# Scores of a chunk moved ahead of the query projection in TensorE's step of a pipelined attention and feed-forward stack

## The chip, the cores and the metric

One core of one Trainium2 chip runs the whole program; the other cores do nothing. Its engines are TensorE (PE, matrix products; PEld is its weight load), VectorE (DVE), ScalarE (ACT), GpSimd (POOL) and SyncE (SP, which only issues DMAs here). The metric is the device time of one execution in microseconds (us), median of the runs, all inputs and outputs in HBM.

## What is computed

`x` is 2048 tokens by 128 features, f32. Four residual layers follow each other: a causal attention (A), a stack (S0), a grouped attention (B), and the same stack again with the same weights (S1). Each stack has depth 6, and each of its layers is, cut to what matters here:

```
for i in range(6):
    x = attn_layer(shift_tokens(x), ...) + x     # 16 heads of 64, windows of 32 tokens, each query
    x = ffn_layer(shift_tokens(x), ...) + x      # window looks at its own and the one before
attn_layer: q, k, v = split(x @ Wqkv); q, k = l2norm * scale, then rotated; k cached per window
            out = softmax(8 q k^T, masked) v;  out @ Wo
ffn_layer:  a, gate = split(layernorm(x) @ W1 + b1);  a * gelu(gate) @ W2 + b2
```

## The kernel before, in words

Features lie on the partitions, tokens on the free axis. A stack works in **chunks** of 128 tokens (16 to a layer, 96 to a stack) and **blocks** of 512 tokens for the feed-forward part (24 to a stack). Every engine runs the same list of steps `k`: 16 written out, a hardware loop over layers 1 to 5 with 16 steps in its body, and some steps at the end that drain the pipeline (`read_steps`, L361). In each step every engine works at several chunks in different stages: `at.chunk(d)` is the chunk `k - d`, or nothing if there is none; `at.block(d)` is a block that falls due in every fourth step. The order in which an engine takes the pieces is written out by hand in its `step`, and each piece begins with waits on counting semaphores; so an engine that waits holds back everything behind that wait.

TensorE's step (L544) is, in the order before:

1. pieces of the feed-forward blocks that come first (L559 to L588), the product with `Wo` of chunk k-4 (L590), more feed-forward pieces (L599 to L616);
2. transposing the probabilities of chunk k-3 into `slot[1]` (L618 to L624; the row names it `slot<-consts,probs` at L538, the line of the helper `turn`);
3. in every fourth step the third gate tile (L626 to L631), in another fourth step the product with `W2` (L633 to L644, the matmuls are L642);
4. the **query projection** of chunk k (L646, `project_in`, matmuls L531 to L533) into `slot[0]`;
5. in every fourth step a value tile (L655), in another the mean of a block (L662, matmul L665);
6. the **value products** of chunk k-3: 128 small matmuls (L668 to L681, matmuls L677);
7. the **scores** of chunk k-2 into `slot[3]`: two matmuls that lay down the mask (L700) and 128 small ones (L707), behind the waits L685 to L697;
8. transposing the rotated queries (L713, L538), the value projection (L719), transposing the attention output `Os` (L726), the key projection (L734), transposing the rotated keys (L742).

Each fourth step of one kind has one piece of the feed-forward part that touches `slot[3]`, and the scores wait for the engine that empties it. Below the four kinds of step are called by that piece: the **variance step** (L565 at its head; the scores wait for `ln_eps`, L689), the **W2 step** (piece L641; they wait for `ln_half` and `f_done`, L691 and L695), the **gelu step** (gates L607, L609, L631; they wait for `gelu_done`, L693) and the **mean step** (L665; they wait for `hid_done`, L697).

The engines that answer to it:

- ScalarE (`act_stack`, L752): copies of `slot[2]` and `slot[1]` to `qT`, `V`, `OT`; `k_copy` (L817); `Exp` of the scores (L822); `kT` (L832); `probsT` (L845); in the gelu step a table load and three `Gelu` (L858, the rows name the whole group `centred<-slot,b`); then `q_copy` (L871).
- VectorE (`dve_stack`, L973): row maximum of the scores (L1001), cosine half of the queries straight from `slot[0]` (L983, signals `aq_done`), normalising the keys (L987), subtracting the maximum (L1021), sums of squares (L1028, L1081), cosine half of the keys, row sums (L1050), residual add (L1063), in the W2 step `XA` (L1114, signals `f_done`), normalising the queries (L987, signals `qn_done`), in the mean step the rotation tables (L1094), `x_lo` (L1130), and last `Os` (L1138, signals `on_done`), which takes the value products from `slot[1]`. The next row maximum stands directly behind `Os`.
- GpSimd: the sine halves (L909), the add to the rotated queries (L925), the inverse norms (L938, L942).
- SyncE copies the values of each chunk into window form (`VW<-V`, L452 to L456) by DMA.

The value projection (L723) and the transpose of `Os` (L728) wait for `on_done`; the key projection (L739) waits for `aq_done`; the query projection of the next step waits for `k_copy` and `ak_done`.

Of the kernel before, what the change touches and what calls it, by code (L numbers as in the profile page):

```python
# [23 lines left out]
NCH = S // 128  # L24
NB = S // 512
DEPTH = 6
H, DH = 16, 64
WIN = 32
# [4 lines left out]
START = 1  # L33
# [57 lines left out]
def build(nc, A, out, place, stages=("A", "S0", "B", "S1")):  # L91
    n_const = A["shape_constants"].shape[1]
    ctx = ExitStack()
    with ctx:
        def sem(name):
            return ctx.enter_context(nc.semaphore(name))

        def sb(name, shape, dt=F32, at=ctx):
            return at.enter_context(nc.sbuf_tensor(name, shape, dt))
# [4 lines left out]
        def const(name):  # L104
            a, n = place[name]
            return consts[:, a:a + n]

        ident = const("ident")
        ident_b = sb("ident_b", [128, 128], BF16)
        mask_qk = sb("mask_qk", [128, 128], BF16)  # L110
        mask_kq = sb("mask_kq", [128, 128], BF16)
        mask_win = sb("mask_win", [128, 2, 2 * WIN], BF16)
# [11 lines left out]
        slot = [ctx.enter_context(nc.psum_tensor(f"slot{i}", [128, 1024], F32)) for i in range(4)]  # L124
# [88 lines left out]
        qT = sb("qT", [128, 8, 128], F32, mem)  # L213
        kT = sb("kT", [128, 8, 160], F32, mem)
# [29 lines left out]
        s = {n: sem(n) for n in names}  # L244
# [126 lines left out]
        class Stage:  # L371
# [13 lines left out]
            def upto(self, c):  # L385
                return self.g + min(max(c + 1, self.lo), self.hi)

            def blocks(self, c):
                return self.f + min(max(c + 1, self.lo), self.hi) // 4
# [129 lines left out]
        def norms_before(call):  # L519

            return (1 + (LN_S0 if call == 0 else LN_S1)) * NB - BLOCKS * call

        def pe_stack(pe, call):
            n0 = norms_before(call)
# [19 lines left out]
            def step(layer, g, f, k, lo, hi):  # L544
                at = Stage(g, f, k, lo, hi)
                upto, blocks = at.upto, at.blocks
# [13 lines left out]
                if b is not None:  # L560
# [4 lines left out]
                    for c in range(4):  # L565
                        mm = pe.matmul(slot[3][:, 512 + c:513 + c], squares[:, 0, c * 128:c * 128 + 128],
                                       const("mean1"), start=True, stop=True)
# [10 lines left out]
                if b is not None:  # L578
# [4 lines left out]
                    for c in range(4):  # L583
                        at_col = 4 * (b % 4) + c
                        mm = pe.matmul(slot[3][:, 128 * c:128 * c + 128],
                                       rstd[:, at_col:at_col + 1].to_broadcast([128, 128]), ident,
                                       start=True, stop=True)
                    mm.then_inc(s["ln_bc"], 1)  # L588

                c = at.chunk(4)  # L590
                if c is not None:
# [3 lines left out]
                    for j in range(8):  # L595
                        mm = pe.matmul(slot[2][:, 512:640], Wo[:, j, :], OT[:, j, :], start=(j == 0), stop=(j == 7))  # L596
# [21 lines left out]
                c = at.chunk(3)  # L618
# [15 lines left out]
                if b is not None:  # L634
# [6 lines left out]
                    for t, (j, a, m) in enumerate(VALUE_TILES):  # L641
                        mm = pe.matmul(slot[3][:, 512:1024], W2[0:m, j, :], hidden[0:m, j, :],  # L642
                                       start=(t == 0), stop=(t == 2))
                    mm.then_inc(s["w2_mm"], 1)  # L644

                c = at.chunk(0)  # L646
                if c is not None:
                    if c == 0:
# [14 lines left out]
                if b is not None:  # L663
                    pe.wait_ge(s["xb_done"], START + 2 * upto(k - 4))
                    pe.matmul(slot[2][:, 512:1024], const("centre128"), XB[:, (b % NB) * 512:(b % NB) * 512 + 512],  # L665
                              start=True, stop=True).then_inc(s["ln_mean"], 1)

                c = at.chunk(3)  # L668
                if c is not None:
# [3 lines left out]
                    for h in range(H):  # L673
                        r = slice(64 * (h % 2), 64 * (h % 2) + 64)
                        col = (h % 2) * 512 + (h // 2) * 64
                        for w in range(4):
                            mm = pe.matmul(slot[1][32 * w:32 * w + 32, col:col + 64],  # L677
                                           probsT[r, h // 2, 32 * w:32 * w + 32],
                                           VW[c % 2][r, w, (h // 2) * 64:(h // 2) * 64 + 64],
                                           start=True, stop=True)  # L680
                    mm.then_inc(s["pv_mm"], 1)  # L681

                c = at.chunk(2)
                if c is not None:
                    pe.wait_ge(s["qT_sb"], START + g + c + 1)  # L685
                    pe.wait_ge(s["kT_sb"], START + g + c + 1)
                    pe.wait_ge(s["sub_done"], START + upto(c - 1))
                    if at.block(5) is not None:
                        pe.wait_ge(s["ln_eps"], START + n0 + blocks(k - 5))  # L689
                    if at.block(6) is not None:  # L690
                        pe.wait_ge(s["ln_half"], START + n0 + blocks(k - 6))  # L691
                    if at.block(7) is not None:
                        pe.wait_ge(s["gelu_done"], START + 3 * blocks(k - 7))  # L693
                    if at.block(10) is not None:
                        pe.wait_ge(s["f_done"], START + 2 * blocks(k - 10))  # L695
                    if at.block(8) is not None:
                        pe.wait_ge(s["hid_done"], START + 3 * blocks(k - 8) - 2)  # L697
                    first = 0 if c % NCH == 0 else 1
                    for i in range(2):
                        pe.matmul(slot[3][:, i * 512:(i + 1) * 512], ident_b[:, :],  # L700
                                  mask_win[:, first:first + 1, :].to_broadcast([128, 8, 2 * WIN]),
                                  start=True, stop=False, skip_group_check=True)
                    for h in range(H):
                        r = 64 * (h % 2)
                        col = (h % 2) * 512 + (h // 2) * 64
                        for w in range(4):
                            mm = pe.matmul(slot[3][32 * w:32 * w + 32, col:col + 64],  # L707
                                           qT[r:r + 64, h // 2, 32 * w:32 * w + 32],
                                           kT[r:r + 64, h // 2, 32 * w:32 * w + 64],
                                           start=False, stop=True, skip_group_check=True)  # L710
                    mm.then_inc(s["s_mm"], 1)

                c = at.chunk(1)  # L713
                if c is not None:
# [4 lines left out]
                c = at.chunk(1)  # L719
# [6 lines left out]
                c = at.chunk(3)  # L726
# [7 lines left out]
                c = at.chunk(0)  # L734
# [7 lines left out]
                c = at.chunk(1)  # L742
                if c is not None:
# [4 lines left out]
                    turn(slot[1], rot_out[1]).then_inc(s["tk_mm"], 1)  # L748

            read_steps(pe, call, step, 10)  # L750

        def act_stack(act, call):  # L752
# [1457 lines left out]
```

## Time and profile before

| | us |
|---|---|
| median of 3 runs | 6616.09 (6614.64 to 6626.6) |
| the profiled execution | 6607.82 |
| its span, first to last instruction | 6606.0 |
| busy TensorE | 5876.7 |
| busy VectorE | 4586.9 |
| busy GpSimd | 4226.5 |
| busy ScalarE | 3394.8 |

By the slices of the page the first attention runs to about 1090 us, the first stack from there to about 2880 us, the grouped attention to about 4750 us, the second stack to the end. Only the two stacks run the changed code. The page's own time (6607.82) is 8.3 us below the median of the runs. A timeline row gives start, duration, engine, line, operation and count, and in brackets how long the engine sat idle before it and what released it; "issue" means that the profile shows nothing it waited for.

### The profile page before, as it was taken

The numbers are of one execution on the slowest core, as the hardware profiler recorded it, in microseconds if no ns is written. First come the engines' busy times: TensorE is split into PE (matmuls) and PEld (weight loads), VectorE is DVE, ScalarE is ACT, GpSimd is POOL, SyncE is SP. The second block draws the span as 40 slices with busy tenths as digits, with TensorE's granted clock in tenths as the row PEclk, the third lists the DMA queues.
The fourth block names the chain that finished last, engine by engine and source line by source line (L and its number), as shares of the span: only waits on it lengthen the run. The fifth ranks groups of instructions, "written<-read, shape, count | busy, mean of one in ns | idle before, by whom it ended". The sixth has DMA issues, their size and how long they took to land. (4 is left out here: it accounts for less than half of the span.)

```text
span 6606.0 us, 186540 instructions
## 1 busy us (share of the span) xinstructions
PE 5876.7 (89%) x75443; PEld 3954.0 (60%) x75443; DVE 4586.9 (69%) x5856; ACT 3394.8 (51%) x4009; POOL 4226.5 (64%) x2048
## 2 busy tenths in 40 slices
PE   8998996888888888879999999999688888888887
PEld 4334334766666666656555555555376666666665
DVE  6345345988888888857656556553388888888886
ACT  1431434666666666633444434443366666666664
POOL 0000005888888888833777777778788788888884
PEclk6665667999999999989999999999899999999999
DMA  0000002222222222210000000000122222222221
GB/s 24 1 1 2 1 1 57 62 71 73 66 64 67 70 64 64 63 28 1 1 1 1 1 1 1 1 1 1 35 62 73 63 70 62 73 65 68 64 66 48
DMA packets 187705, 254.28 MB, mean 38 GB/s; under 512 B 60348, under 2 KB 81336, under 8 KB 186680
## 3 DMA queue, kind: packets, MB, share of 16 engines
q1 hardware_dynamic: 186840, 242.02, 14.1%
q8 instruction: 631, 10.34, 0.7%
q14 instruction: 234, 1.92, 0.1%
HBM read 38.98 MB, written 1.57 MB: 6 GB/s over the span
## 5 line engine op out<-in xcount | busy, mean ns | idle before, releaser
L1937 POOL TENSOR_TENSOR XB<-XB,Pb 128x1024 f32<-128x1024 f32 x448 | 1070.1, 2389 | 338.6 <-ACT Pb L1897 297.7
L909 POOL TENSOR_TENSOR sin_qk<-raw_qk,rot 128x512 f32<-128x512 f32 x768 | 1002.7, 1327 | 78.5 <-ACT raw_qk L817 48.4
L1947 DVE TENSOR_REDUCE b_pmax<-slot 128x1 f32<-128x512 f32 x1024 | 653.6, 683 | 325.1 <-PE slot L1684 324.1
L1897 ACT ACTIVATE Pb<-slot 128x1024 f32<-128x1024 f32 x512 | 502.6, 1024 | 702.1 <-PE slot L1795 647.9
L925 POOL TENSOR_TENSOR rot_out<-rot_out,sin_qk 128x1024 f32<-128x1024 f32 x192 | 600.4, 3127 | 396.5 <-DVE rot_out L983 395.5
L942 POOL TENSOR_TENSOR inv_norm<-norm2c,minus_half 128x16 f32<-128x16 f32 x192 | 668.2, 3480 | 171.4 <-DVE norm2c L1084 171.1
L282 POOL TENSOR_TENSOR rstd<-variance,minus_half 128x4 f32<-128x4 f32 x20 | 19.8, 1008 | 1075.6 <-DVE variance L291 1075.5
L531 PE MATMUL slot<-w_hi,x_hi 128*128 128x512 f32 x1152 | 543.9, 472 | 69.6 <-POOL w_lo L900 46.7
L782 ACT ACTIVATE qT<-slot 128x1024 f32<-128x1024 f32 x192 | 197.1, 1027 | 745.6 <-PE slot L538 745.6
L938 POOL TENSOR_TENSOR inv_norm<-norm2c,minus_half 128x16 f32<-128x16 f32 x192 | 559.3, 2913 | 0.0
L983 DVE TENSOR_TENSOR rot_out<-slot,rot 128x1024 f32<-128x1024 f32 x384 | 468.8, 1221 | 71.8 <-PE slot L538 41.4
L707 PE MATMUL slot<-kT,qT 64*32 64x64 f32 x24576 | 332.5, 228 | 192.9 <-issue 192.8
L1807 PE MATMUL slot<-Pb,Vb 128*64 128x512 f32 x2048 | 495.9, 605 | 1.1 <-ACT Pb L1897 1.1
L538 PE MATMUL slot<-consts,rot_out 128*128 128x128 f32 x3072 | 429.2, 284 | 57.1 <-issue 36.3
L987 DVE TENSOR_TENSOR rot_out<-rot_out,inv_norm 128x1024 f32<-128x1024 f32 x384 | 475.2, 1237 | 6.5 <-POOL inv_norm L938 5.2
L1682 PE MATMUL slot<-KA,QA 128*128 128x512 f32 x1024 | 462.0, 451 | 13.5 <-DVE b_pmax L1947 8.1
L533 PE MATMUL slot<-w_hi,x_lo 128*128 128x512 f32 x1152 | 464.8, 404 | 0.0
L532 PE MATMUL slot<-w_lo,x_hi 128*128 128x512 f32 x1152 | 464.5, 403 | 0.0
L707 PEld LDWEIGHTS slot<-kT,qT 64*32 64x32 f32 x24576 | 271.9, 107 | 303.5 <-issue 303.3
L538 PEld LDWEIGHTS slot<-consts,rot_out 128*128 128x128 f32 x3072 | 359.0, 145 | 114.8 <-issue 75.4
L1793 PE MATMUL slot<-QA,KA 128*128 128x512 f32 x1024 | 411.4, 402 | 5.7 <-ACT Pb L1897 5.7
L1684 PE MATMUL slot<-KB,QB 66*128 66x512 f32 x1024 | 408.5, 399 | 0.0
(212 smaller groups left out, 13260.1 us busy)
## 6 DMA issues: line engine op xcount, KB each, us to landing
VW<-V SPq DMA_DIRECT2D x1152, 128.0 KB
VW<-V SPq DMA_DIRECT2D x768, 64.0 KB
w_raw<-in_Wqkv SPq DMA_DIRECT2D x36, 512.0 KB, 3.6
Wo<-in_Wo SPq DMA_DIRECT2D x12, 512.0 KB, 4.2
W<-in_W SPq DMA_DIRECT2D x12, 341.0 KB, 3.2
consts<-in_shape_constants SPq DMA_DIRECT2D x1, 2436.5 KB, 8.9
QB<-rows_dram SPq DMA_DIRECT2D x128, 2.0 KB
W<-in_W SPq DMA_DIRECT2D x24, 64.0 KB
```

What stands on the lines that cost most here:

```text
L531: pe.matmul(out, x_hi[ring][:, :], w_hi[:, cols], start=True, stop=False)
L538: mm = pe.transpose(o[:, j * 128:(j + 1) * 128], src[:, j * 128:(j + 1) * 128], ident)
L707: mm = pe.matmul(slot[3][32 * w:32 * w + 32, col:col + 64], qT[r:r + 64, h // 2, 32 * w:32 * w + 32], kT[r:r + 64, h // 2, 32 * w:32 * w + ...
L909: ins = pool.tensor_tensor(dst[:, :, x, :], src[:, :, 1 - x, :], tab, ALU.mult)
L925: pool.tensor_tensor(rot_out[0][:, :], rot_out[0][:, :], rot_sin[0], ALU.add)\
L938: pool.tensor_tensor(inv_norm[0][:, :], norm2c[0][:, :], minus_half[:, 0:H], ALU.pow)\
L942: pool.tensor_tensor(inv_norm[1][:, :], norm2c[1][:, :], minus_half[:, 0:H], ALU.pow)\
L987: dve.tensor_tensor(v, v, inv_norm[i][:, :].unsqueeze(2).to_broadcast([128, H, DH]), ALU.mult)\
L1807: mm = pe.matmul(slot[3][64 * hh:64 * hh + 64, 0:512], Vb[p // 2 % 2][:, k, :], Pb[:, at % B_RING, 512 * hh:512 * hh + 512], start=(k == 0 ...
L1897: act.activation(Pb[:, at % B_RING, :], slot[n % 2][:, :], ACT.Exp).then_inc(s["b_exp"], 1)
L1937: pool.tensor_tensor(b_sum[:, window % 2, :], Pb[:, (at - 1) % B_RING, :] if k == 1 else b_sum[:, window % 2, :], Pb[:, at % B_RING, :], A ...
L1947: dve.tensor_reduce(b_pmax[:, n // 2, u:u + 1], o[:, 512 * x:512 * x + 512], AX.X, ALU.max)\
```

## The change

In TensorE's step the piece "scores" (7 in the list) is put directly in front of the query projection (4), that is behind 2 and 3. Its waits, its matmuls and its signal are the same. Nothing is added or removed; no other engine's list changes. The query projection, the fourth-step pieces of 5 and the value products follow it in their old order, and behind the value products comes the transpose of the queries.

```diff
                     mm.then_inc(s["w2_mm"], 1)
 
+                c = at.chunk(2)
+                if c is not None:
+                    pe.wait_ge(s["qT_sb"], START + g + c + 1)
+                    pe.wait_ge(s["kT_sb"], START + g + c + 1)
+                    pe.wait_ge(s["sub_done"], START + upto(c - 1))
+                    if at.block(5) is not None:
+                        pe.wait_ge(s["ln_eps"], START + n0 + blocks(k - 5))
+                    if at.block(6) is not None:
+                        pe.wait_ge(s["ln_half"], START + n0 + blocks(k - 6))
+                    if at.block(7) is not None:
+                        pe.wait_ge(s["gelu_done"], START + 3 * blocks(k - 7))
+                    if at.block(10) is not None:
+                        pe.wait_ge(s["f_done"], START + 2 * blocks(k - 10))
+                    if at.block(8) is not None:
+                        pe.wait_ge(s["hid_done"], START + 3 * blocks(k - 8) - 2)
...
+                    mm.then_inc(s["s_mm"], 1)
+
                 c = at.chunk(0)
                 if c is not None:
...
                     project_in(slot[0], c % 4, 0).then_inc(s["q_mm"], 1)
...
                 c = at.chunk(3)
...
                     mm.then_inc(s["pv_mm"], 1)
 
-                c = at.chunk(2)
...
-                    mm.then_inc(s["s_mm"], 1)
-
                 c = at.chunk(1)
                 if c is not None:
                     pe.wait_ge(s["qn_done"], START + g + c + 1)
                     wait_for_slot2()
                     turn(slot[2], rot_out[0]).then_inc(s["tq_mm"], 1)
```

## Rows read from the trace of the kernel before

**Rows 1.** The page: busy time of the engines, share of the span, instructions

```profile
PE 5876.7 (89%) x75443; PEld 3954.0 (60%) x75443; DVE 4586.9 (69%) x5856; ACT 3394.8 (51%) x4009; POOL 4226.5 (64%) x2048
```

**Rows 2.** Window of four steps: length, busy PE, PEld, DVE, ACT, POOL, clock, DMA

```profile
2387.64:2460.22 72.58, 64.65 (x1333) 50.48 (x1332) 63.22 (x79) 48.32 (x57) 59.72 (x30) 1.00 0.27 70
```

**Rows 3.** Groups of PE, 1922 to 2832 us (busy, mean ns, idle before)

```profile
L538 PE MATMUL slot<-consts,rot_out 128*128 128x128 f32 x760 | 108.0, 287 | 16.2 <-issue 13.2
...
L707 PE MATMUL slot<-kT,qT 64*32 64x64 f32 x6144 | 85.0, 231 | 47.7 <-issue 47.6
...
L677 PE MATMUL slot<-VW,probsT 64*32 64x64 f32 x6144 | 72.1, 225 | 5.3 <-issue 5.3
```

**Rows 4.** Waits, 1200 to 2800 us (total us, times, longest)

```profile
PE slot L707 <- issue: 82.4, 77, 3.4
...
PE slot L566 <- issue: 13.0, 4, 3.4
...
DVE row_max L1001 <- PE slot L707: 108.7, 56, 4.3
```

**Rows 5.** Instruction fetches by DMA, 2387 to 2461 us

```profile
q8 instruction: 11, 0.18, 1.0%
```

**Rows 6.** Timeline of PE over four steps, variance, W2, gelu, mean

```profile
2388.43 0.47 PE L531 MATMUL slot<-w_hi,x_hi 128*128 128x512 f32 x1
...
2389.90 1.02 PE L542 MATMUL slot<-normed,W 128*128 128x512 f32 x2
2390.86 1.49 PE L677 MATMUL slot<-VW,probsT 64*32 64x64 f32 x128
...
2396.70 0.48 PE L531 MATMUL slot<-w_hi,x_hi 128*128 128x512 f32 x1
...
2405.15 2.75 PE L642 MATMUL slot<-normed,W 128*128 128x512 f32 x6
...
2415.35 0.48 PE L531 MATMUL slot<-w_hi,x_hi 128*128 128x512 f32 x1
...
2423.50 1.04 PE L538 MATMUL slot<-consts,probs 128*128 128x128 f32 x8
...
2428.88 0.60 PE L700 MATMUL slot<-mask_win,ident_b 128*128 128x512 bf16 x2 [0.62 <-ACT centred L858]
...
2431.76 0.41 PE L707 MATMUL slot<-kT,qT 64*32 64x64 f32 x18 [1.01 <-issue]
...
2432.27 1.09 PE L538 MATMUL slot<-consts,rot_out 128*128 128x128 f32 x8
...
2452.02 0.50 PE L531 MATMUL slot<-w_hi,x_hi 128*128 128x512 f32 x1 [0.99 <-DVE Os L1138]
```

**Rows 7.** Timeline of DVE over the same steps

```profile
2395.77 1.23 DVE L1001 TENSOR_REDUCE row_max<-slot 128x16 f32<-128x1024 f32 x1 [0.76 <-PE slot L707]
2408.48 1.53 DVE L1114 SCALAR_TENSOR_TENSOR XA<-slot,ffn_cols,XB 64x512 f32<-64x512 f32 x2
...
2428.55 1.23 DVE L1138 TENSOR_TENSOR Os<-slot,row_inv 128x1024 f32<-128x1024 f32 x1 [0.60 <-PE slot L677]
2432.23 1.23 DVE L1001 TENSOR_REDUCE row_max<-slot 128x16 f32<-128x1024 f32 x1 [2.46 <-PE slot L707]
...
2450.74 1.23 DVE L1138 TENSOR_TENSOR Os<-slot,row_inv 128x1024 f32<-128x1024 f32 x1
...
2467.35 1.21 DVE L1138 TENSOR_TENSOR Os<-slot,row_inv 128x1024 f32<-128x1024 f32 x1
2468.49 1.21 DVE L1001 TENSOR_REDUCE row_max<-slot 128x16 f32<-128x1024 f32 x1
```

**Rows 8.** Timeline of ACT: the three gelus of the gelu step

```profile
2426.99 1.83 ACT L858 ACTIVATE centred<-slot,b 128x512 f32<-128x512 f32 x3
```

**Rows 9.** One long gap of PE and its clock: window, then timeline

```profile
2032.00:2040.00 8.00, 5.38 (x143) 4.65 (x143) 4.00 (x5) 1.70 (x2) 2.50 (x4) 0.79 0.07 14
...
2035.42 1.25 PE L707 MATMUL slot<-kT,qT 64*32 64x64 f32 x79 [2.62 <-issue]
```

More of the change, by code:

```diff
@@ L644, in step @@
                     mm.then_inc(s["w2_mm"], 1)
+                c = at.chunk(2)
[13 more added lines that the diff above has]
+                        pe.wait_ge(s["hid_done"], START + 3 * blocks(k - 8) - 2)
+                    first = 0 if c % NCH == 0 else 1
+                    for i in range(2):
+                        pe.matmul(slot[3][:, i * 512:(i + 1) * 512], ident_b[:, :],
+                                  mask_win[:, first:first + 1, :].to_broadcast([128, 8, 2 * WIN]),
+                                  start=True, stop=False, skip_group_check=True)
+                    for h in range(H):
+                        r = 64 * (h % 2)
+                        col = (h % 2) * 512 + (h // 2) * 64
+                        for w in range(4):
+                            mm = pe.matmul(slot[3][32 * w:32 * w + 32, col:col + 64],
+                                           qT[r:r + 64, h // 2, 32 * w:32 * w + 32],
+                                           kT[r:r + 64, h // 2, 32 * w:32 * w + 64],
+                                           start=False, stop=True, skip_group_check=True)
+                    mm.then_inc(s["s_mm"], 1)
                 c = at.chunk(0)
@@ L681, in step @@
                     mm.then_inc(s["pv_mm"], 1)
-                c = at.chunk(2)
[L684 to L710, printed above, removed]
-                    mm.then_inc(s["s_mm"], 1)
                 c = at.chunk(1)
```

## The prediction

> **What bounds the kernel now.** The page comes first: TensorE is busy 89% of the span, VectorE 69%, GpSimd 64% [rows 1]. Two thirds of it are stacks, and only they run the changed code, so the window of four steps (one of each kind) is next: of 72.58 us TensorE is busy 64.65, VectorE 63.22, GpSimd 59.72, ScalarE 48.32 [rows 2]. No engine is full; the order of their waits sets the pace.
>
> The groups of TensorE count 6144 score matmuls in 910 us. At 128 to a step that is 48 steps of 18.96 us, or 75.8 us for a cycle of four. The same groups hold most of TensorE's idle time: 47.6 us before L707, 5.3 before L677, 13.2 before the transposes, all put down to "issue", that is to nothing the profile shows; per cycle (47.6 + 5.3 + 13.2) / 12 = 5.5 us [rows 3]. In the list of waits the gap at L707 occurs 77 times in some 85 steps, longest 3.4 us; and VectorE waits 108.7 us for the scores [rows 4].
>
> I read these gaps as instruction supply. One cycle issued 1333 matmuls and 1332 weight loads [rows 2] while 11 packets fetched 0.18 MB of instructions [rows 5]: a packet of 16 KB for about 240 instructions of TensorE. Value products and scores are 512 small instructions back to back, two packets' worth in 4 us; the gap then falls inside a run of L707, as the one of 2.62 us with 79 of 128 scores left [rows 9]. The rule of the Trainium skill speaks against this reading: Runtime: NRT & Kernel Launch, section Instruction fetch mechanics, says that TensorE buffers 2048 instructions, refilled in blocks of 256, and that crossing a block is mostly hidden; the trace shows the gap in nearly every step. By that rule the gaps would have another cause and stay, which is the first rival.
>
> **What the change removes.** Scores and value products are now parted by the query projection, 12 instructions (matmuls and weight loads) in 1.47 us (2388.43 to 2389.90) [rows 6]. Between one packet's end in the scores and the next one's in the value products lie about 3.0 us (256 small instructions at 1.49, and 1.47) in place of 2.0 (1.49 and the mask). With gaps of about 1.0 to 1.3 now, supply needs some 3.1 to 3.3 us. Gain: 5.5 us a cycle, less what remains; I take 0.8 (twice 0.4, in the steps where it isn't covered), between 0 and 1.5.
>
> **What it adds.** Two waits that the query projection and the value products used to cover. The chain that closes over a cycle goes from one `Os` to the next, because `Os` needs the value products, stands in front of the row maximum on VectorE, and releases the value projection.
>
> *Variance step's Os to W2 step's.* VectorE: `Os` to row maximum 1.14 (2467.35 to 2468.49), row maximum to the end of `XA` 14.24 (2395.77 to 2410.01), 15.4 together [rows 7]. TensorE would be ready before: value projection 1.28 after `Os` began (2450.74 to 2452.02) [rows 6, 7], from there to the end of W2 11.20 (2396.70 to 2407.90) [rows 6], 12.5 together. So the scores wait about 2.9 us for `f_done`, with the query projection, the value products and the query transpose queued behind. Then scores 2.38 (2428.88 to 2432.27 less the gap of 1.01) [rows 6], projection 1.47, value products 1.49, hand-overs 0.2: 5.5. Sum 20.9.
>
> *W2 step's to gelu step's.* 1.28 to the value projection, 8.15 from it to the transpose of probabilities (2415.35 to 2423.50) [rows 6], 5.32 from there to the end of the gelus (2423.50 to 2428.82) [rows 6, 8]. That is 14.75. Before, projection and value products ran under the gelus and the scores waited 0.62. Now everything waits some 3.5 us; then 5.5. Sum 20.3.
>
> *Gelu step's to mean step's.* Row maximum to `Os` 18.51 (2432.23 to 2450.74) [rows 7], plus 1.14, less 0.7: the key projection, with it exp, comes that much sooner after the row maximum, as the scores are long done. 19.0.
>
> *Mean step's to variance step's.* 16.6, VectorE without idle time (2450.74 to 2467.35) [rows 7]; the move changes nothing, and its gap costs nothing. The remaining waits of the scores are met by then (`hid_done` comes within about 1.3 us of the transpose, `ln_eps` before it).
>
> Sum 76.8. Before, 75.8 holds the turn of the loop (L566, 13.0 us at 4 turns, 0.8 a cycle [rows 4]), so 75.0 compares: **+1.8** a cycle without supply gaps. Of that 5.5 is gained and 7.3 lost.
>
> **The clock.** A gap of 2.62 us stands in a window in which the clock was granted at 0.79 over 8 us [rows 9]: 8 x 0.21 = 1.7 us of full clock lost, 3.4 us at 1.2 GHz instead of 2.4. The new waits of 2.9 and 3.5 us are longer, twice a cycle. The small matmuls suffer less than in proportion: 79 scores behind that gap took 1.25 us [rows 9], 15.8 ns each, where 128 value products take 1.49, 11.6 ns each. As half of what follows the waits is such work, I take 0.7 for each, 1.4 a cycle. Bounds: 3.4 (both in full), and below nothing, -0.5, as gaps that brought such falls go.
>
> Nothing else has a price. GpSimd's sine half of the queries waits for `q_copy`, later by up to 4 us, but its next piece waits for `aq_done`, which is later still; its 59.72 us [rows 2] leave room. The window copies by DMA have two steps until their use. ScalarE idles where `q_copy` is late.
>
> **Sum.** 1.8 + 0.8 + 1.4 = 4.0 us a cycle. Scores meet these waits for 22 of the 24 blocks of a stack (the last two fall behind the last scores): 44 cycles, +176 us, on 6607.8 of the profiled execution 6784. The median of the runs stands 8 us above it: 6790.
>
> **The rivals.**
> 1. *The gaps aren't supply and stay.* Then 5.5 of gain is missing and the residual 0.8 goes: 44 x (4.0 + 5.5 - 0.8) = 383, about 7000. For: the skill's rule; against: packets and run lengths fit.
> 2. *Faster: `XA` is done when the scores come.* Place: L695. If VectorE's 15.4 falls under TensorE's 12.5, because TensorE runs later than by my sum or VectorE's instructions get shorter, the wait of 2.9 and its clock loss vanish. 1.8 - 2.9 - 0.5 = -1.6, 44 times -70: about 6545. It decides from 2.9 us less on VectorE; with 14.2 us of gapless instructions I see no way.
> 3. *Cancelled.* The cost of the gelu wait shrinks by slack elsewhere to what supply gains: 6616.
>
> **How the numbers follow.** Forecast 0.80; rival 1 0.07; rival 2 0.08; rival 3 0.05. Range: low with supply and clock at their ends, 44 x (1.8 - 0.5) = 57, 6673 with the median's 8, a little lower for errors of hand schedules; high 44 x (1.8 + 1.5 + 3.4) = 295, 6911, all at its worst. I give 6655 to 6900; rivals 1 and 2 are outside. Over 0.2% (13 us, about what a measurement tells from no change) faster 0.08, the same 0.05, slower 0.87.
>
> **What would show it.** Right: L707 loses most of its "issue"; L700 waits for `XA` by 2 to 3 us and for the gelus by 3 to 4 us once per cycle; VectorE's wait before the row maximum is gone, and `Os` waits for L677 instead; L531 (value projection) waits for `Os` in most steps; the cycle is 79 to 80 us; the granted clock in the stacks is below 0.97. Wrong: "issue" unchanged (rival 1), or no wait for `XA` (rival 2).

## The result, and the profile after

| | before | after |
|---|---|---|
| median of 4 runs, us | 6621.35 (6614.64 to 6633.0) | 6936.62 (6922.65 to 6946.74) |
| ratio to before | | 1.0473, 95% interval 1.0448 to 1.0498 |
| the profiled execution, us | 6607.82 | 6946.74 |
| its span, us | 6606.0 | 6944.9 |
| granted clock over the span | 0.918 | 0.896 |

The change makes the kernel 315 us slower by the medians, and 339 by the two profiled executions. The forecast was +174 with a range to 6900: the right side, the size too small by almost half. The kernel before was measured again beside every batch of experiments, and its median moved between 6617 and 6635 us; the ratios below are each taken within a batch, and a ratio times 6621 us gives the differences. In the kernel after, the mask is L663, the scores L670 and the value products L707; all other lines that are named here keep their numbers.

The page of the kernel after, busy times of the engines, against [rows 1]:

```profile
PE 6060.2 (87%) x75443; PEld 4027.6 (58%) x75443; DVE 4641.8 (67%) x5856; ACT 3395.4 (49%) x4009; POOL 4206.1 (61%) x2048
```

The work is the same, and so are the counts. TensorE is busy 184 us more with the same 75443 matmuls: the same work takes longer, which is what a lower clock looks like. VectorE is busy 55 us more, with no instruction added. That second sign is easily passed over, and a cause behind it turned out to be worth about a third of the loss. (By the records it is 115 us more in one instruction, L1031, and 41 us less in another, L1130.)

The groups of TensorE in the kernel after, over the same stretch as [rows 3] (1922 to 2832 us):

```profile
L538 PE MATMUL slot<-consts,rot_out 128*128 128x128 f32 x704 | 94.0, 276 | 13.5 <-issue 6.7 <-DVE rot_out L987 3.1 <-DVE normed L1151 1.7
...
L670 PE MATMUL slot<-kT,qT 64*32 64x64 f32 x5632 | 79.0, 269 | 0.4 <-issue 0.4
...
L707 PE MATMUL slot<-VW,probsT 64*32 64x64 f32 x5597 | 67.1, 226 | 0.8 <-issue 0.7
```

5632 scores are 44 steps or 11 cycles where there were 12: 910 / 11 = 82.7 us a cycle. What stood before the scores as "issue" in [rows 3], 47.6 us, is 0.4. Over the three groups 6.7 + 0.4 + 0.7 = 7.8 us are left, 0.7 a cycle.

The waits of the kernel after, 1200 to 2800 us, against [rows 4] (total us, times, longest):

```profile
DVE Os L1138 <- PE slot L707: 265.0, 59, 8.0
...
PE slot L663 <- ACT centred L858: 65.5, 20, 3.3
...
PE slot L663 <- DVE XA L1114: 64.5, 19, 3.6
...
PE slot L531 <- DVE Os L1138: 20.2, 63, 0.5
...
PE slot L542 <- DVE XB L1063: 14.4, 20, 0.7
```

The two new waits are there, once a cycle each: 64.5 / 19 = 3.4 us for `XA` and 65.5 / 20 = 3.3 us for the gelus. VectorE's 108.7 us of waiting before the row maximum [rows 4] has become 265.0 us before `Os`. And there is a wait that I had not expected, 0.7 us of the third gate tile (L542) for `XB` once a cycle.

One cycle of TensorE in the kernel after, the W2 step and the gelu step (timeline, only the rows used):

```profile
2519.80 1.03 PE L663 MATMUL slot<-mask_win,ident_b 128*128 128x512 bf16 x2 [3.54 <-DVE XA L1114]
2520.77 2.05 PE L670 MATMUL slot<-kT,qT 64*32 64x64 f32 x128
...
2537.32 1.09 PE L542 MATMUL slot<-normed,W 128*85 128x512 f32 x2 [0.73 <-DVE XB L1063]
...
2541.71 1.03 PE L663 MATMUL slot<-mask_win,ident_b 128*128 128x512 bf16 x2 [3.31 <-ACT centred L858]
2542.68 2.05 PE L670 MATMUL slot<-kT,qT 64*32 64x64 f32 x128
2544.66 0.79 PE L531 MATMUL slot<-w_hi,x_hi 128*128 128x512 f32 x1
```

The reader sees what a wait of 3.3 to 3.5 us leaves behind: the mask takes 1.03 us where it took 0.60 [rows 6], the 128 scores 2.05 where 79 of them took 1.25 even behind a gap [rows 9], a matmul of the projection 0.79 for 0.47 [rows 6]. The windows of both stretches give the clock (start and end, length, busy PE, PEld, DVE, ACT, POOL, clock, DMA):

```profile
2519.00:2529.00 10.00, 8.78 (x279) 6.53 (x280) 5.04 (x6) 3.59 (x4) 4.58 (x3) 0.83 0.01 3
2541.00:2550.00 9.00, 8.19 (x272) 6.04 (x272) 1.28 (x3) 2.74 (x4) 3.31 (x3) 0.67 0.01 2
```

The mean clocks of 0.83 and 0.67 are a mixture of 1.2 and 2.4 GHz: by the durations it is low behind the wait, while the mask, the scores and a part of the projection run.

The same steps on VectorE in the kernel after (timeline):

```profile
2503.76 1.22 DVE L1138 TENSOR_TENSOR Os<-slot,row_inv 128x1024 f32<-128x1024 f32 x1 [0.79 <-PE slot L707]
...
2510.77 1.10 DVE L1031 TENSOR_SCALAR norm2c<-norm 128x16 f32<-128x16 f32 x1
...
2518.22 1.53 DVE L1114 SCALAR_TENSOR_TENSOR XA<-slot,ffn_cols,XB 64x512 f32<-64x512 f32 x2
...
2526.14 1.23 DVE L1138 TENSOR_TENSOR Os<-slot,row_inv 128x1024 f32<-128x1024 f32 x1 [4.93 <-PE slot L707]
...
2549.16 1.23 DVE L1138 TENSOR_TENSOR Os<-slot,row_inv 128x1024 f32<-128x1024 f32 x1 [7.72 <-PE slot L707]
```

From `Os` to `Os` the W2 step takes 22.38 us here and the gelu step 23.02; the forecast had 20.9 and 20.3. And one small instruction stands out: the clamp of the queries' squared norms, L1031, on 128x16 elements, takes 1.10 us.

### The profile page after: what moved, and what is told of

It reads as the page before. It is cut to its first block and busy times, and to the rows that moved or that the text cites. A ratio compares the mean times of both kernels' runs of the same rounds, so it can differ in the third digit from the quotient of the medians.

```text
span 6944.9 us, 186540 instructions
## 1 busy us (share of the span) xinstructions
PE 6060.2 (87%) x75443; PEld 4027.6 (58%) x75443; DVE 4641.8 (67%) x5856; ACT 3395.4 (49%) x4009; POOL 4206.1 (61%) x2048
## 5 line engine op out<-in xcount | busy, mean ns | idle before, releaser
L909 POOL TENSOR_TENSOR sin_qk<-raw_qk,rot 128x512 f32<-128x512 f32 x768 | 967.3, 1281 | 525.8 <-ACT raw_qk L871 521.5
L942 POOL TENSOR_TENSOR inv_norm<-norm2c,minus_half 128x16 f32<-128x16 f32 x192 | 683.0, 3557 | 236.9 <-DVE norm2c L1084 236.8
L1138 DVE TENSOR_TENSOR Os<-slot,row_inv 128x1024 f32<-128x1024 f32 x192 | 234.9, 1224 | 649.1 <-PE slot L707 648.3
L871 ACT ACTIVATE raw_qk<-slot 128x1024 f32<-128x1024 f32 x192 | 196.4, 1023 | 825.8 <-PE slot L533 825.8
L938 POOL TENSOR_TENSOR inv_norm<-norm2c,minus_half 128x16 f32<-128x16 f32 x192 | 559.3, 2913 | 0.0
L532 PE MATMUL slot<-w_lo,x_hi 128*128 128x512 f32 x1152 | 478.9, 416 | 0.1
L538 PE MATMUL slot<-consts,rot_out 128*128 128x128 f32 x3072 | 413.2, 277 | 48.9 <-DVE rot_out L987 18.0
L663 PE MATMUL slot<-mask_win,ident_b 128*128 128x512 bf16 x384 | 147.2, 474 | 315.5 <-DVE XA L1114 147.5
L538 PEld LDWEIGHTS slot<-consts,rot_out 128*128 128x128 f32 x3072 | 345.0, 141 | 111.0 <-issue 64.6
```

Of the source, the lines that this page charges most:

```text
L532: pe.matmul(out, x_hi[ring][:, :], w_lo[:, cols], start=False, stop=False)
L538: mm = pe.transpose(o[:, j * 128:(j + 1) * 128], src[:, j * 128:(j + 1) * 128], ident)
L909: ins = pool.tensor_tensor(dst[:, :, x, :], src[:, :, 1 - x, :], tab, ALU.mult)
L938: pool.tensor_tensor(inv_norm[0][:, :], norm2c[0][:, :], minus_half[:, 0:H], ALU.pow)\
L942: pool.tensor_tensor(inv_norm[1][:, :], norm2c[1][:, :], minus_half[:, 0:H], ALU.pow)\
```

## The experiments

Two theories entered. That of the forecast: supply gaps go where scores and value products are parted, and the two exposed waits cost more than that, with the clock's fall behind them. Its rival: the parting itself, or what it moves on other queues, is what costs, in every kind of step, and the waits are incidental. The pieces of TensorE's step were made local functions, so that their order could be chosen by `k % 4` (0 the variance step, 1 W2, 2 gelu, 3 mean).

**Which steps lose.** In the first run the two steps with a wait keep the old order, in the second only they have the new one, in the third only the gelu step keeps the old one.

(Condensed: the pieces stand line by line in the kernels.)

```diff
+                def old(): query_projection(); value_tile(); value_products(); scores()
+                def new(): scores(); query_projection(); value_tile(); value_products()
+                (old if k % 4 in (1, 2) else new)()      # first run
+                (new if k % 4 in (1, 2) else old)()      # second
+                (old if k % 4 == 2 else new)()           # third
```

> Scores ahead of the query projection in the variance and mean steps alone; W2 and gelu steps in the old order. If the loss is all in the two exposed waits (theory), the supply gaps of the two moved steps go and nothing is added: a few per cent below before is not possible in a VectorE-bound mean step, so 6621 less 48 cycles x 1 to 2 us, 6530 to 6580 us. If delaying the query projection and the value products costs by itself in every step (rival), slower than before: over 6650 us.

> The complement: scores ahead only in the W2 and gelu steps. Theory of the exposed waits: all of the loss and more, as the gain of the other two steps is missing: 6980 to 7060 us. Rival (cost in every step): about half of the whole change's 315 us, near 6780 us.

> The changed kernel with only the gelu step back in the old order. Price of the gelu step alone: in the traces it went from about 18.8 to 24.2 us, 5.4 us x 44 = 240 us, so 6700 us. If the gelu wait cost only the 2.7 us of the prediction's terms, 44 x 2.7 = 120 us, 6815 us.

| new order in | median, us | ratio, 95% interval |
|---|---|---|
| variance, mean | 6546.33 | 0.9874 (0.9849 to 0.9899) |
| W2, gelu | 6966.66 | 1.0508 (1.0481 to 1.0535) |
| variance, mean, W2 | 6720.94 | 1.0134 (1.0108 to 1.0161) |
| all (the change) | 6936.62 | 1.0473 (1.0448 to 1.0498) |

By the ratios, the move in the variance and mean steps, where no wait is exposed, brings (0.9874 - 1) x 6621 = -83 us; the W2 step's move costs (1.0134 - 0.9874) x 6621 = +172, the gelu step's +224. The rival is out: half of the change is a gain. Of the expectations the first held, the second was passed by a little on the cheap side (6967 for 6980 at least), and the third had 6700 for 6721. The waits of the first run (there the mask is L704, the scores L711), 1200 to 2800 us:

```profile
PE slot L711 <- issue: 44.5, 42, 2.7
...
PE slot L704 <- DVE XA L1129: 13.9, 18, 1.1
...
PE slot L704 <- ACT centred L873: 13.7, 20, 0.7
```

The gap at the scores has gone from 82.4 us, 77 times [rows 4] to 44.5 us, 42 times: about half of the steps, as half of them were parted; and no wait is longer than 1.1 us.

**Are the gaps supply?** The kernel before, with 40 transposes (80 instructions, matmul and weight load) ahead of everything on TensorE, written to a tile that is overwritten later. If a gap belongs to a place in the stream of instructions, it must move forward in the program by 40 pairs.

```diff
+            for _ in range(40):
+                pe.transpose(slot[0][:, 0:128], x_nat[:, 0, :], ident)
```

> The kernel before with 40 more transposes (80 instructions) at the start of TensorE's program, outside the stacks. If the gap stands where a block of instructions ends, the long gap of the loop's sixth step moves from between score 49 and 50 of 128 to 40 pairs earlier, between 9 and 10, and likewise all others; the time changes by under 1%. If the gap comes from a semaphore, a DMA or the array, it stays between 49 and 50.

The kernel before, the same step in two turns of the loop, 299 to 303 us apart (timeline of PE):

```profile
2336.17 0.72 PE L707 MATMUL slot<-kT,qT 64*32 64x64 f32 x49
...
2340.30 1.39 PE L707 MATMUL slot<-kT,qT 64*32 64x64 f32 x79 [3.40 <-issue]
...
2639.36 0.72 PE L707 MATMUL slot<-kT,qT 64*32 64x64 f32 x49
...
2643.51 1.39 PE L707 MATMUL slot<-kT,qT 64*32 64x64 f32 x79 [3.42 <-issue]
```

The kernel with 40 transposes ahead:

```profile
2351.65 0.32 PE L707 MATMUL slot<-kT,qT 64*32 64x64 f32 x9
2352.80 1.40 PE L707 MATMUL slot<-kT,qT 64*32 64x64 f32 x119 [0.84 <-issue]
...
2656.26 0.32 PE L707 MATMUL slot<-kT,qT 64*32 64x64 f32 x9
2657.41 1.41 PE L707 MATMUL slot<-kT,qT 64*32 64x64 f32 x119 [0.83 <-issue]
```

Before, the scores of this step break after the 49th in every turn. With the shift they break after the 9th, 40 pairs earlier, in the two turns shown, and have no gap in the other three. The other steps follow (72 for 112, 30 for 70): in 131 steps of the kernel before the longest gap is over 0.4 us and can move by 40 inside its run; with the shift it is found 40 pairs earlier in 120 of them, there is none in 11, and it stands elsewhere in none. Data and semaphores are the same, only the place in the stream of instructions moved. The records of the DMA queue that fetches instructions close the argument: each of the 168 gaps over 0.4 us inside the scores of the kernel before ends 1.2 to 1.6 us after a packet of instructions has landed, with 6.8 us from one packet to the next on average. The gaps are instruction supply. The Trainium skill (Runtime: NRT & Kernel Launch, section Instruction fetch mechanics) says that crossing a block is mostly hidden; this case's traces differ: here it costs up to 3.4 us where two blocks of small matmuls follow each other. The kernel as a whole took 6601.03 us in its one run, which can't be told from no change.

**What the clock costs.** The change, with two extra query projections (their result is overwritten by the real one) ahead of the scores' waits in the W2 and gelu steps, so that TensorE works where it idled.

```diff
+                if k % 4 in (1, 2) and at.chunk(0) is not None:
...
+                    for _ in range(2):
+                        project_in(slot[0], c % 4, 0)
```

> The changed kernel, and in the W2 and gelu steps two extra query projections (12 matmuls, about 2.9 us of work, overwritten by the real one) stand in front of the scores' waits, where TensorE idles 3.5 and 3.3 us. If the clock after those idle times is what the prediction undersized, the low clock goes and the time falls by 2 to 3 us a cycle in spite of the added work: 6800 to 6850 us. If the clock does not matter, 6930 to 6990 us.

It took 6882.34 us, ratio 1.0377 (1.0352 to 1.0402): 54 us less than the change by the medians, 64 by the ratios, with more work. The expected time, 6800 to 6850, was missed. Windows from 1500 to 2500 us, the change:

```profile
1500.00:2500.00 1000.00, 844.43 (x16147) 643.46 (x16147) 792.18 (x959) 592.24 (x686) 736.15 (x361) 0.93 0.24 62
```

and with the filler:

```profile
1500.00:2500.00 1000.00, 895.72 (x16635) 686.02 (x16634) 808.85 (x972) 602.84 (x699) 747.94 (x367) 0.99 0.24 63
```

The clock is 0.99 for 0.93. So the fall of the clock is real and costs more than I had given it (the table below), but it is not the whole of the surplus. The filler also brings something back. Its waits for nothing that the profile shows, 1200 to 2800 us (value products L680, scores L711), and behind them those of the change (L707, L670):

```profile
PE slot L680 <- issue: 15.0, 37, 1.0
...
PE slot L711 <- issue: 12.2, 15, 1.4
```

```profile
PE slot L670 <- issue: 3.8, 6, 1.1
...
PE slot L707 <- issue: 3.5, 7, 0.9
```

Without the slow stretch the small matmuls run out of instructions again: 27.2 us of gaps for 7.3, 1.0 a cycle.

**An order that should have both.** Value products first, then the query projection, then the scores: parted, and with everything ahead of the waits. (The diff is condensed again.)

```diff
+                value_products(); query_projection(); value_tile(); scores()                # first run
+                                                                                            # second run:
+                if k % 4 in (1, 2): value_products(); query_projection(); value_tile(); scores()
+                else: scores(); query_projection(); value_tile(); value_products()
```

> Order in every step: value products, query projection, scores. Scores and value products are parted as in the change, but the scores stay last, so their two waits stay covered. If the gaps are instruction supply, L707's issue time falls by more than half as in the changed kernel and the time falls, less what the value products now wait for probsT (about 1 us in three steps of four): 6520 to 6620 us. If parting them does nothing, over 6650 us.

> Variance and mean steps as in the change, W2 and gelu steps with value products, query projection, scores. If supply gaps and exposed waits are the two terms, this has neither and beats the 6546 us of the version with two steps in the old order: 6470 to 6530 us. If the value products' wait for probsT costs what the gaps give, 6540 to 6600 us.

The first missed: 6652.17 us over ten runs, ratio 1.0028 (1.0013 to 1.0043), no gain and a trace of a loss. The waits of TensorE's matmuls, 1200 to 2800 us (value products L680, scores L711):

```profile
PE slot L680 <- DMA VW<-V: 36.8, 34, 1.4
...
PE slot L680 <- ACT probsT L854: 28.0, 20, 1.4
PE slot L680 <- issue: 21.2, 12, 2.8
PE slot L711 <- issue: 19.6, 16, 1.7
PE slot L538 <- issue: 14.2, 16, 2.7
```

The gaps did go, as expected: at the scores from 82.4 us, 77 times [rows 4] to 19.6 us, 16 times. The four groups of small matmuls together (mask, scores, value products, transposes) have 55.0 us of "issue", where the kernel before has 122.0, the 82.4 and these:

```profile
PE slot L538 <- issue: 18.2, 18, 2.4
...
PE slot L700 <- issue: 12.0, 22, 1.8
PE slot L677 <- issue: 9.4, 6, 2.0
```

What took the gain are the value products' own operands. Moved to the front, they wait 36.8 us for the window copies by DMA and 28.0 us for `probsT`, 64.8 us together, none of which stands among the waits before; against 67.0 us of gaps gained that fits the unchanged time. It is read from the traces; the next run bears on it. I had reckoned with `probsT` and not with the copies. The second run uses each order where it is good (in the W2 and gelu steps the product with `W2` or the third gate tile stands ahead of the value products and covers most of that wait: 4.7 us are left for the copies), and it took 6509.87 us, ratio 0.9806 (0.9783 to 0.983): faster than the kernel before by 125 us, and than the change by over 400. It lies in its expected range.

**The slow clamp.** The sum still lacked time in the two chains ahead of the waits, and VectorE's busy time pointed to L1031. Its group, 1200 to 2800 us, kernel before:

```profile
L1031 DVE TENSOR_SCALAR norm2c<-norm 128x16 f32<-128x16 f32 x85 | 37.1, 437 | 10.8
```

and after:

```profile
L1031 DVE TENSOR_SCALAR norm2c<-norm 128x16 f32<-128x16 f32 x77 | 81.6, 1059 | 9.8
```

The mean of 437 ns is no duration that occurs: one L1031 takes either 0.17 us or about 1.1 (0.8 to 2.2). By the records of both stacks it is slow 54 times in 192 before and 182 in 192 after; each of the 182 times an instruction of GpSimd is running (169 times L909), and the clamp ends just after it. The GpSimd row beside the clamp of 2510.77 above, kernel after:

```profile
2510.58 2.50 POOL L909 TENSOR_TENSOR sin_qk<-raw_qk,rot 128x512 f32<-128x512 f32 x2
```

and before, in the same kind of step, GpSimd:

```profile
2401.85 2.51 POOL L909 TENSOR_TENSOR sin_qk<-raw_qk,rot 128x512 f32<-128x512 f32 x2 [0.26 <-ACT raw_qk L817]
```

and VectorE:

```profile
2401.73 0.17 DVE L1031 TENSOR_SCALAR norm2c<-norm 128x16 f32<-128x16 f32 x1
```

Before, the clamp began 0.12 us ahead of GpSimd's multiply and was through; after, it begins 0.19 us behind and has to sit out the first of the two, 2510.58 to about 2511.9. The Trainium skill (SBUF — State Buffer, section Who interferes with whom) has the rule: VectorE and GpSimd share a pair of ports which one of them locks for its whole instruction; `tensor_scalar` can need it, `tensor_reduce` on trn2 doesn't. The traces agree: `tensor_scalar` was slow in 182 of 192 steps of the change, and as a reduction (below) in none. That suggests the test: first the clamp left out (of the change; this kernel doesn't clamp the queries' squared norms at 1e-24, nothing else is left out), then written as a reduction by maximum over pairs of norm and constant, on the kernel before and on the change. The edit of the reduction changes the clamp of the keys (L1084) in the same way, of which the diff shows nothing; that one was slow once in 192 steps in either kernel, so it can't carry the effect.

```diff
-        norm2 = [sb(f"norm2_{i}", [128, H], F32, mem) for i in range(2)]
+        norm2 = [sb(f"norm2_{i}", [128, H, 2], F32, mem) for i in range(2)]    # second column is 1e-24
...
-                    dve.tensor_scalar(norm2c[0][:, :], norm2[0][:, :], 1e-24, None, ALU.max).then_inc(s["nq_done"], 1)
+                    dve.tensor_reduce(norm2c[0][:, :], norm2[0][:, :, :], AX.X, ALU.max).then_inc(s["nq_done"], 1)
```

> The changed kernel without VectorE's clamp of the queries' sums of squares at 1e-24 (L1031, a 128x16 instruction; the sums go straight to GpSimd). In the traces it takes 1.1 us in 182 of 192 steps after the change and in 54 before, and ends with a GpSimd instruction (L909). If that collision is the part of the loss that the prediction lacked, the time falls by 192 x 1.1 x the share that lies on the chain, half or more: 80 to 180 us, 6760 to 6850 us. If it is covered, under 30 us: 6905 or more.

> The kernel before with the clamp of the sums of squares done by a reduction over pairs (sum, 1e-24) with max, in place of TENSOR_SCALAR; the same values. If the clamp is slow by a collision with GpSimd that the other form of instruction does not have, the 54 slow ones of 192 (1.1 us in place of 0.18) go: 54 x 0.93 = 50 us of VectorE, 10 to 40 of it in the time: 6580 to 6615 us. If the reduction collides as well, no change: 6621 to 6640.

> The changed kernel with the clamp as a reduction. All work of the changed kernel is done, so the 87 us that leaving the clamp out gave should come back nearly in full if the collision (182 of 192) is the cause: 6840 to 6870 us. If leaving the instruction out was the cause, 6920 or more.

| | median, us | ratio, 95% interval |
|---|---|---|
| change without the clamp | 6849.98 | 1.0318 (1.0294 to 1.0342) |
| change, clamp as a reduction | 6832.43 | 1.0325 (1.0303 to 1.0346) |
| before, clamp as a reduction | 6605.83 | 0.9991 (0.9976 to 1.0007) |

The group in the change with the reduction:

```profile
L1031 DVE TENSOR_REDUCE norm2c<-norm 128x16 f32<-128x32 f32 x80 | 14.9, 186 | 9.9
```

It is never slow, although it reads twice as much. By the ratios the collision costs the change (1.0473 - 1.0325) x 6621 = 98 us (103 with the clamp left out, the same within the intervals; the reduction had been expected to give back 87 at most, and gave somewhat more), and the kernel before nothing that can be measured: its 6605.83 lies in the expected range only because that batch ran faster (6617 for the kernel before), and 10 to 40 us of gain had been expected. It is a cost that the change brings with it although it touches neither engine's list.

**Both together**, with the filler on the change, and with the mixed order.

> The changed kernel with the clamp as a reduction and with the filler projections in the two waits. If collision (87) and clock (55) are separate terms, their sum: 6937 - 87 - 55 = 6795 us, 6780 to 6815. If the low clock hid the collision or the reverse, 6830 or more.

> The mixed order (6510 us) with the clamp as a reduction: a version meant to beat both kernels. 6440 to 6490 us if the collision also lies on its chain; 6500 to 6520 if VectorE's Os-to-Os stretch is not what ends last there.

The first took 6810.32 us, ratio 1.0289 (1.0268 to 1.031): only 22 us below the same without the filler (24 by the ratios), where the filler had brought 64 alone. The two remedies don't add up, although the time lies in the expected range; that sum had too little for the collision. Two parts of it are in the records. With the clamp as a reduction the wait for `XA` is shorter (51.5 us for 64.5, 19 times), and less is lost to the clock behind the waits, 2.5 us a cycle for 3.0, so the filler has less to give back. And the filler delays the mean step's `Os` by 0.65 us in the change and by 0.83 with the reduction, where the gaps inside that step's scores grow from 0.30 to 0.88 us and from 0.71 to 1.42 us: supply gaps again. The second took 6487.37 us, ratio 0.9801 (0.9774 to 0.9827), the fastest kernel of this study; but against 0.9806 without the reduction nothing is gained, although the clamp was slow there in 118 of 192 steps, which is in keeping with the kernel before, where the collision costs nothing either. The expected 6440 to 6490 was met by a faster batch alone. The page of it, to be held against [rows 1]:

```profile
PE 5892.2 (91%) x75443; PEld 3940.2 (61%) x75443; DVE 4508.6 (70%) x5860; ACT 3398.8 (52%) x4009; POOL 4199.6 (65%) x2048
```

The same matmuls in 168 us less of TensorE than in the change, and every engine busier as a share.

## Why the prediction was right in kind and short in size

The terms of the sum against what the records show, as means over the 42 cycles of both stacks that can be followed from the `Os` of a variance step to the next (us):

| from, to | forecast | after | clamp as reduction | with filler | both |
|---|---|---|---|---|---|
| `Os` of variance step, end of `XA` | 15.4 | 16.07 | 15.37 | 16.10 | 15.42 |
| end of `XA`, `Os` of W2 step | 5.5 | 6.74 | 6.51 | 5.88 | 5.95 |
| `Os`, transpose of probabilities | 9.43 | 9.45 | 9.51 | 9.52 | 9.53 |
| transpose, end of gelus | 5.32 | 6.08 | 5.35 | 6.01 | 5.35 |
| end of gelus, `Os` of gelu step | 5.5 | 7.08 | 6.87 | 5.81 | 5.78 |
| `Os`, `Os` of mean step | 19.0 | 19.07 | 18.90 | 19.72 | 19.73 |
| `Os`, `Os` of variance step | 16.6 | 18.53 | 18.23 | 18.30 | 18.11 |
| sum | 76.8 | 83.02 | 80.74 | 81.35 | 79.88 |

Before, the same mean cycle is 75.50 us. The change adds 7.5 a cycle, 44 cycles 331 us, of the 339 of the profiled executions. The forecast was 4.0: 76.8, with 0.8 for supply and 1.4 for the clock, against 75.0.

*What the change removes.* Right. The gap at the scores is gone, 0.7 us a cycle of "issue" is left where I took 0.8, and the shift of 40 pairs with the landings of the packets shows that it was supply. Both are better proof than the counting of packets on which I had relied. Rival 1 is out. (The stacks are 55% of the span, 1090 to 2880 and 4750 to 6606 us, not the two thirds that the prediction says; the sum doesn't use that.)

*What it adds, place and order.* Right: both waits, `Os` behind the value products, the value projection behind `Os` (63 times), the chain of every term. The term from `Os` to the transpose of the probabilities was met within 0.1, that to the mean step's `Os` within 0.1. Rivals 2 and 3 are out; `XA` came even later than by my sum.

*The two chains of 15.4 and 5.32, too short by 0.7 and 0.8 (a cost that was put at nothing).* Here the step "row maximum to the end of `XA` 14.24" failed: I read it from one cycle in which L1031 took 0.17 us and took the durations as fixed while I moved the engines against each other. In the change the clamp nearly always meets GpSimd's multiply. It delays `XA` directly, and in the gelu step through `XB`, for which the third gate tile waits 0.7 us, and the gelus wait for that; with the reduction the wait for `XB` is gone from the list. With it the two terms are 15.37 and 5.35, my numbers to within 0.05. The whole cycle gets 2.3 us shorter, not only these 1.4: the rest comes off the terms behind them, 0.4 of it where less is lost to the clock. "Nothing else has a price" was the wrong sentence: a queue that isn't delayed is still moved in time against its neighbour. The hint stood in the kernel before: a mean of 437 ns for an instruction whose timeline row says 0.17 us.

*The clock and the residual supply.* Here a term of the sum was mis-sized. The stretches behind the waits took 6.74 + 7.08 = 13.8 for 11.0, where I had 1.4 of clock and 0.8 of supply on top. By the records the mask, the scores and the projection behind the two waits take 10.3 us a cycle in the change and 7.3 with the filler, whose mean clock is 0.99: the low clock costs 3.0, 1.3 behind the wait for `XA` and 1.7 behind that for the gelus, for the 0.7 each of the forecast. That is still inside its bounds of -0.5 to 3.4, near the upper one. The mistake is the discount by half. I had it from 79 scores behind one gap of 2.62 us, 15.8 ns each, and the 128 scores behind the longer waits took 2.05 us, 16.0 ns each, much the same; but the slow stretch also takes in the mask (1.03 for 0.60) and, in the gelu step above all, the projection (0.79 for 0.47 a matmul). Supply, on the other hand, costs 0.2 in these stretches and not 0.8: the value products are slower by that much than their usual 1.48, and no more. And the 5.5 for the rest was 0.2 too long each. The three errors partly cancel, which is luck: 0.6 is left. With the filler the two terms are 5.88 + 5.81 = 11.7, as the value products, with gaps in them, then take 1.0 a cycle more than their usual.

*Mean step to variance step, 18.53 for 16.6.* A plain error of reading. I took one cycle without a gap (16.61); the mean in the kernel before is 18.04. A minimum of one term was set against a mean of the whole. What the mean holds above the minimum is the turn of the loop, in 8 of the 42 cycles: there the step takes 24.10 us in the change and 21.84 before, in the others 17.22 and 17.14. One such turn in the change, PE and then the window over it:

```profile
1666.73 1.86 PE L566 MATMUL slot<-consts,squares 128*128 128x1 f32 x8 [2.71 <-issue]
1668.45 3.76 PE L596 MATMUL slot<-OT,Wo 128*128 128x128 f32 x16
```

```profile
1663.00:1673.00 10.00, 7.29 (x34) 6.47 (x35) 6.50 (x9) 4.17 (x5) 7.34 (x4) 0.66 0.54 149
```

The gap of 2.7 us is followed by a low clock (0.66), at which the 16 matmuls of L596 take 3.76 us, where their usual is 1.95. So the turn costs 1.3 us a cycle in the change and 0.9 before, where I had counted its gap alone, 0.8, and left it out on both sides. The other cycles hold 0.6 above 16.6. Before, supply gaps in the transposes account for some of that, as the value projection starts 2.10 us after `Os` on average and not 1.28; in the change it starts after 1.35, so there the 0.6 has another cause, which stays open. Net of the 0.5 by which the cycle before (75.5) stood above my 75.0, this term accounts for 1.4 of what is missing.

So the missing 3.5 is, term by term, 1.4 in the two chains with the collision, 1.4 of the mean step's term, 0.6 of clock and supply, 0.1 in the gelu to mean term. Taken out by experiment instead, the collision is worth 2.3 (98 to 100 us), because it also lengthens the waits and what follows them. The forecast's ends took in the clock but neither of the first two, which is why the result lies outside.

## What to carry to other kernels

Before a piece with a late operand is moved forward, list what is behind it: the work that it passed is the work that hid its wait, and where the wait exists only in some steps, the order can differ by step (6510 us for 6937 and 6621). The same holds for a piece that is moved to the front: value products ahead of everything lost to their own operands (64.8 us) what they gained in supply (67.0 us). When queues shift against each other, the durations are not constants: look for instructions whose mean is far from their timeline row, see what runs on the neighbouring engine when they are slow, and price them in both states. And take the terms of a cycle's sum from the same kind of average as the cycle that they are set against.

## What the hardware did that I had not expected

- A `TENSOR_SCALAR` of 128x16 elements, SBUF to SBUF, takes 0.17 us alone and about 1.1 us when a GpSimd multiply of two SBUF operands has begun just before; a `TENSOR_REDUCE` of twice the input took 0.186 us and was never slow, in four kernels. In the pair of rows above a start that is 0.3 us later decides it; over the whole kernel the collision was worth 98 us. L1130, with two inputs in SBUF, moved the other way: slow in 44 of 192 steps before and in 5 after. It is slow in 5 with the reduction too, so it has no part in the 98 us; what it is worth by itself was not tested.
- Two blocks of small matmuls in a row cost TensorE a gap of up to 3.4 us (1.1 on average), at a place that is fixed in the stream of instructions and mostly repeats in every turn of the loop. Each of 168 such gaps ended 1.2 to 1.6 us after a packet of instructions had landed.
- An idle time of 3.3 to 3.5 us is followed by some us at the lower clock, and costs 1.3 and 1.7 us more in this kernel. Two query projections of no use in that idle time took the mean clock from 0.93 to 0.99 and made the kernel 54 us faster by the medians, although at full clock supply gaps of 1.0 us a cycle came back.

Left open: what the mean to variance step holds above 16.6 us in the change beside the turn of the loop, and why its turns are 2.3 us longer than before.
